# The two lone GRU passes of a four-layer GNN kernel, with their block loops written out

## The reference

```python
gi = a @ W_ih.T + b_ih              # a: the messages summed over each node's edges
gh = h @ W_hh.T + b_hh
i_r, i_z, i_n = split(gi, 3); h_r, h_z, h_n = split(gh, 3)
r = sigmoid(i_r + h_r); z = sigmoid(i_z + h_z)
n = tanh(i_n + r * h_n)
h_new = (1 - z) * n + z * h
```

## Time and profile before

| | us |
|---|---|
| median of 3 runs | 5424.33 (5411.29 to 5428.64) |
| the profiled execution's own time | 5421.28 |
| its span, first to last instruction | 5419.5 |
| the first dense aggregation ends, the first lone GRU begins | 1542.2 |
| its last POOL operation; the next dense stage begins on PE | 1631.8; 1632.7 |
| the last lone GRU begins, with DVE's put(0) | 5326.5 |
| its last DVE operation ends; the output transfer is issued | 5413.4; 5413.7 |

### The profile page before, as it was taken

The page is one execution under the profiler, slowest core; times in us unless marked ns, Lnnn a source line. Parts: engine busy times, 40 slices in busy tenths (PEclk is TensorE's granted clock), DMA queues, the critical chain, the costliest instruction groups (busy, mean ns, idle before and its releaser), DMA issues. The chain is left out here.

```text
span 5419.5 us, 89480 instructions
## 1 busy us (share of the span) xinstructions
PE 3373.2 (62%) x24458; PEld 2518.9 (46%) x24459; DVE 2843.3 (52%) x7137; ACT 944.6 (17%) x2120; POOL 1974.9 (36%) x2334
## 2 busy tenths in 40 slices
PE   4526777776979989989624444444544444445456
PEld 3412333333979988989513332333333333333345
DVE  8976887776553411332324444444554444445565
ACT  3521246664011200001100000000000000000002
POOL 4670000000021111111365655656665555555550
PEclk5558998888999999999655555555555555555557
DMA  3000011112524444544212222222222222222220
GB/s 130 2 3 13 25 47 59 59 59 99 197 70 143 148 153 156 186 158 154 77 41 52 54 53 51 54 52 55 58 57 55 53 53 53 53 52 60 57 59 22
DMA packets 173577, 404.19 MB, mean 75 GB/s; under 512 B 47902, under 2 KB 109481, under 8 KB 172809
## 3 DMA queue, kind: packets, MB, share of 16 engines
q1 hardware_dynamic: 52409, 259.35, 13.4%
q10 hardware_dynamic: 69360, 91.59, 6.2%
q0 software_dynamic: 51680, 51.82, 5.4%
HBM read 359.52 MB, written 43.07 MB: 74 GB/s over the span
## 5 line engine op out<-in xcount | busy, mean ns | idle before, releaser
L704 POOL DMA_INDIRECT scr<-ptable,src_i x1566 | 1520.6, 971 | 1086.0 <-POOLq L702 617.8
L1151 PE MATMUL ps_all<-stat_w,scr 128*128 128x392 fp8e4 x2712 | 615.4, 363 | 255.3 <-PEq L1155 147.2
L964 PE MATMUL ps_all<-arena 128*128 (+1 forms) x1854 | 351.8, 363 | 676.5 <-PEq L962 332.2
L673 POOL COPY late<-late 128x256 f32<-128x256 f32 (+1 forms) x65 | 25.9, 398 | 1980.8 <-POOLq L671 1980.8
L975 PE MATMUL ps_all<-arena 128*128 128x192 bf16 x1854 | 382.3, 360 | 524.1 <-issue 380.7
L967 PE MATMUL ps_all<-sb_w_e,arena 64*128 64x128 f32 x1854 | 530.6, 441 | 233.9 <-issue 233.4
L1042 PE MATMUL ps_all<-scr,arena 128*128 128x192 bf16 x7203 | 611.1, 247 | 66.9 <-PEq L1040 66.9
L1042 PEld LDWEIGHTS ps_all<-scr,arena 128*128 128x128 fp8e4 x7203 | 600.1, 98 | 76.7 <-issue 74.8
L964 PEld LDWEIGHTS ps_all<-arena 128*128 128x128 bf16 x1854 | 227.0, 137 | 809.8 <-issue 798.7
L912 ACT ACTIVATE arena<-arena 128x384 f32<-128x384 f32 x309 | 161.6, 523 | 2499.1 <-ACTq L911 2114.0
L975 PEld LDWEIGHTS ps_all<-arena 128*128 128x128 bf16 x1854 | 230.2, 143 | 695.6 <-issue 687.8
(11 more groups left out here) (305 smaller groups left out, 3620.2 us busy)
## 6 DMA issues: line engine op xcount, KB each, us to landing
arena<-a_dram SPq DMA_DIRECT2D x245, 784.0 KB, 4.4
arena<-low_dram ACTq DMA_DIRECT2D x309, 192.0 KB
a_dram<-arena SPq DMA_DIRECT2D x49, 784.0 KB, 3.3
arena<-in_e32g ACTq DMA_DIRECT2D x309, 96.0 KB
scr<-ptable,src_i POOLq DMA_INDIRECT x1566
arena<-in_e16p SPq DMA_DIRECT2D x1, 13387.5 KB, 35.3
x<-in_x_nm SPq DMA_DIRECT2D x1, 1664.0 KB, 8.3
out_nm<-x SPq DMA_DIRECT2D x1, 1664.0 KB
```

Source lines behind the costliest of these rows:

```text
L704: pool.indirect_dma_start(grow[:, g % RING, j, :], None, ptable, bass.IndirectOffsetOnAxis(ap=src_i[:, g * GC + j:g * GC + j + 1], axis=0) ...
L964: pe.matmul(z[:, j // 2, j % 2 * 3 * H:(j % 2 + 1) * 3 * H], onehotT[:, m, j * P:(j + 1) * P], qsp[:, ds(t, 1), :], start=j % 2 == 0, stop ...
L1151: return pe.matmul(bank_w[i][:, 0:WC], oh_lo[u][:, j, :], oh_hi[u][:, j, :], **{"start": False, "stop": False, **flags})
```

## The change

The loops over pairs of blocks in both lone GRUs are replaced by Python loops that write out all 13 blocks on PE, ACT and DVE. Addresses and semaphore values become constants. The body on each engine changes:

```diff
-WARM = 16
 # ACT
+                turned(0)
+                turned(1)
+                for b in range(NB):
+                    sigmoid((ps_g, ps_g_odd)[b % 2])
+                    if b + 2 < NB:
+                        turned(b + 2)          # copy_uT, copy_hT of block b + 2
+                    tanh()
 # PE
-                    gate_products(k, odd)
-                    for i in range(WARM):
-                        pe.matmul(ps_a[:, 0:P], ident_h[:, :], ident_h[:, :], start=True, stop=True)
-                    turned()
-                    if more:
-                        front(True, True)
+                for b in range(NB):
+                    if b == NB - 1:
+                        pe.wait_ge(s_cdd, 1)
+                        pe.sem_inc(s_cdd, -1)
+                    gate_products(k, b % 2 == 1)
+                    if b + 1 < NB:
+                        turned()
+                    if b + 2 < NB:
+                        front(True, True)
 # DVE
+                def step(ins):
+                    steps[0] += 1
+                    ins.then_inc(s_v, 1)
+                    v.wait_ge(s_v, steps[0])
+                def put(b):
+                    v.tensor_copy(stage[:, :, :], rows(pair, b))
+                    v.tensor_copy(hstage[:, :, 0:H], rows(h, b))
+                    v.tensor_copy(hstage[:, :, H + 2:HX], rows(aux_s, b)).then_inc(s_stg, 1)
+                def block(b):
+                    g = (ps_g, ps_g_odd)[b % 2]
+                    v.wait_ge(s_rz, 1)
+                    v.sem_inc(s_rz, -1)
+                    step(v.tensor_tensor(cand[:, :, :], rz[:, :, 0:H], g[:, :, 3 * H:], ALU.mult))
+                    v.tensor_tensor(cand[:, :, :], cand[:, :, :], g[:, :, 0:H], ALU.add).then_inc(s_cd, 1)
+                    if b + 3 < NB:
+                        stage_free()
+                        put(b + 3)
+                    v.wait_ge(s_th, 1)
+                    v.sem_inc(s_th, -1)
+                    if b == NB - 3:
+                        v.sem_inc(s_cdd, 1)
+                    step(v.tensor_tensor(dif[:, :, :], rows(h, b), cand[:, :, :], ALU.subtract))
+                    step(v.tensor_tensor(dif[:, :, :], dif[:, :, :], rz[:, :, H:], ALU.mult))
+                    v.sem_inc(s_rzf, 1)
+                    if k == 0:
+                        step(v.tensor_tensor(rows(h, b), dif[:, :, :], cand[:, :, :], ALU.add))
+                        v.wait_ge(s_qf, 1)
+                        v.sem_inc(s_qf, -1)
+                        v.tensor_scalar(qblk, rows(h, b), SCALE, None, ALU.mult).then_inc(s_hb, 1)
+                    else:
+                        step(v.tensor_tensor(dif[:, :, :], dif[:, :, :], cand[:, :, :], ALU.add))
+                        step(v.tensor_tensor(rows(x, b), rows(x, b), dif[:, :, :], ALU.add))
+                put(0)
+                for b in (1, 2):
+                    stage_free()
+                    put(b)
+                for b in range(NB):
+                    block(b)
+                v.sem_inc(s_v, -steps[0])
```

More of the change, by code:

```diff
@@ L410, in gnn @@
         s_cd = sem("s_cd")
+        s_cdd = sem("s_cdd")
         s_th = sem("s_th")
@@ L727, in copy_hT, with sigmoid @@
                 act.copy(to[:, :], ps_m[0:HX, :]).then_inc(s_hT, 1)
-            def gates(g):
+            def sigmoid(g):
                 act.wait_ge(s_gt, 1)
@@ L735, in gates, with tanh @@
                 act.activation(rz[:, :, :], g[:, :, H:3 * H], ACT.Sigmoid).then_inc(s_rz, 1)
+            def gates(g):
+                sigmoid(g)
+                tanh()
+            def tanh():
                 act.wait_ge(s_cd, 1)
@@ L741, in gru, with turned @@
                 act.preload_act_table(ACT.Sigmoid)
[L743 to L748, removed]
-                    if more:
[L750 to L759, removed]
+                def turned(b):
+                    copy_uT((uT, uT_odd)[b % 2])
+                    copy_hT((hT, hT_odd)[b % 2])
+                turned(0)
[4 more added lines that the diff above has]
+                        turned(b + 2)
+                    tanh()
             def split(parts, rows, rest, scale=1.0):
@@ L1015, in gru @@
             def gru(k):
-                def block(odd, more=True):
-                    gate_products(k, odd)
-                    for i in range(WARM):
-                        pe.matmul(ps_a[:, 0:P], ident_h[:, :], ident_h[:, :], start=True, stop=True)
-                    turned()
-                    if more:
-                        front(True, True)
                 front(True, True)
@@ L1472, in gru, with rows @@
             def gru(k):
-                def put(b):
-                    link(v.tensor_copy(stage[:, :, :], block_of(pair, b)))
-                    put_rows(b)
+                steps = [0]
+                def rows(buf, b):
+                    return buf[:, b * TB:(b + 1) * TB, :]
+                def step(ins):
+                    steps[0] += 1
+                    ins.then_inc(s_v, 1)
+                    v.wait_ge(s_v, steps[0])
                 def stage_free():
@@ L1480, in stage_free @@
                     v.sem_inc(s_stgf, -1)
-                def block(b, odd, more=True):
-                    if more:
-                        stage_free()
-                        put(b + 2)
-                    candidates(ps_g_odd if odd else ps_g)
-                    mixed(b)
+                def put(b):
+                    v.tensor_copy(stage[:, :, :], rows(pair, b))
+                    v.tensor_copy(hstage[:, :, 0:H], rows(h, b))
+                    v.tensor_copy(hstage[:, :, H + 2:HX], rows(aux_s, b)).then_inc(s_stg, 1)
@@ L1488, in block @@
                     if k == 0:
-                        link(v.tensor_tensor(block_of(h, b), dif[:, :, :], cand[:, :, :], ALU.add))
-                        to_split(b)
-                    else:
-                        add_to_x(b)
+                        step(v.tensor_tensor(rows(h, b), dif[:, :, :], cand[:, :, :], ALU.add))
+                        v.wait_ge(s_qf, 1)
+                        v.sem_inc(s_qf, -1)
+                        v.tensor_scalar(qblk, rows(h, b), SCALE, None, ALU.mult).then_inc(s_hb, 1)
+                    else:
+                        step(v.tensor_tensor(dif[:, :, :], dif[:, :, :], cand[:, :, :], ALU.add))
+                        step(v.tensor_tensor(rows(x, b), rows(x, b), dif[:, :, :], ALU.add))
```

## The result

The changed kernel takes 5383.58 us in the median of five runs (5379.28 to 5393.30), the kernel before 5423.33 (5411.29 to 5428.64): a ratio of 0.9926, with a 95% interval of 0.9908 to 0.9945. The profiled execution after is 5383.6 us long (span 5381.8), that of before 5421.3 (5419.5).

The account below looks back on a forecast made before the run. DVE's queue, with its waits and bookkeeping, was taken as the bound; 20.5 us from the last GRU and 12.4 from the first made 32.9 off 5421.3, so 5388.4 (5391.4 from the median; forecast 5390), range 5377 to 5409.

Parts of the forecast that it names:

- the bounds of the parts: Both lone GRUs together: the parts' limits were said to give 27.6 to 36.6 us less, so 5385 to 5397.
- the tail: Last GRU's final steps, behind mult 12: forecast to save 0.2 us.
- What bounds the old kernel: DVE's queue, not an engine's work: Lone GRUs before the change: DVE's queue, with its waits and bookkeeping, sets 5.8 us a block.
- The step of 0.50: DVE's linked step in the last GRU: 0.57 us with the decrement, taken as 0.50 with the counted wait.
- Last GRU, balance of PE and DVE at 4.05 a block: Last lone GRU: DVE and PE both near 4.0 us, mult 0 to mult 12 48.4 against 69.8.
- 0.5 off for fetching code: Last GRU: 0.5 us struck from the gain of 21 because written-out blocks are more instruction blocks to fetch.
- Prologues unchanged: Stretch before the first mult of each lone GRU: no change, PE at the low clock there.
- First GRU: POOL becomes the bound at 4.85: First lone GRU: POOL paces blocks at 4.85 us, before 5.87, for a gain of 12.4.
- Exclusion of DVE and POOL: Rival, first GRU: SBUF operations hold each other off, 5.45 us a block, total gain 25.7, 5397; 15%.
- The fall of the clock: Rival, PE in both GRUs: without fillers the clock falls, 24 us more in each GRU, 5469; 4%.
- The late-front rival: Rival: put waits for ACT's copy behind a late front, periods near 5.5, 8 us less in all, 5415; 5%.
- Its own signs of being wrong: Last GRU's blocks over 4.6 us, first not paced by POOL, or anything outside both stretches moving over 3 us.

Follow-up runs that it names:

- E2: Kernel before with its three loops over pairs of blocks written out, nothing else: first lone GRU 63.05 us, last 62.76, in all 5423.43.
- E3: Changed kernel with counted steps turned back into wait for 1 and decrement: first GRU 58.97 us, last 50.20.
- E8: Changed kernel with PE transposing three tiles of four in the last GRU from block 3 on: last 44.59 us, first 58.01, in all 5390.91.
- E12: Kernel before with the fillers (unread PE products) dropped, nothing else: mult 0 to mult 12 of last GRU 70.98 us, of first 74.85, in all 4760.27.
- E10: Kernel before with loops written out and fillers dropped: last GRU 62.71 us, first 64.47.
- E1: Changed kernel with the 16 filler products put back behind each block's gate products: first GRU 58.12 us, last 56.92, in all 5403.23.
- E6: Changed kernel with POOL's split in five operations instead of six, its first copy of qblk gone: first GRU 51.44 us, in all 5379.68.
- E7: E6 with POOL's loop of the first GRU also written out: first 49.08 us, last 46.70, in all 5368.35, ratio to the kernel before 0.9891.
- E5: Changed kernel with the put two blocks ahead, before the candidates: first GRU 67.71 us, last 66.26, in all 5407.99.
- E9: Changed kernel with the put two blocks ahead, before the candidates, and ACT's old order: first GRU 60.36 us, last 56.35, in all 4734.05.
- E4: Changed kernel with ACT's old order (sigmoid, tanh, then copies): first GRU 57.86 us, last 47.79, in all 5407.25.
- E11: E7 with unread products where PE would wait ahead of the lone GRUs: 4699.94 us, ratio to the kernel before 0.9887.

## Why the prediction was right, point by point

The profiled execution was forecast at 5388.4 and took 5383.6; 32.9 us were to go, 37.8 went. That is more than the bounds of the parts allowed (36.6; their lower sum is 28.1, not 27.6), and the surplus lies in the last GRU: 24.7 went, 20.5 were forecast, 22 were its limit. The 4.2 us are a longer fall of mult 0 to mult 12 (1.7), the prologue (1.2), a slip in the sum (21.4 and 0.2 are 21.6, not 21: 0.6), the 0.5 for fetching code and the tail (0.2). So the place of the gain and its mechanism were right, and the total came within the stated 5377 to 5409 by the allowance for the spread of the runs. By its own steps:

- *What bounds the old kernel: DVE's queue, not an engine's work.* Right. E2 took 7 us out with no operation changed, by turning a loop into constants, and DVE's rows there close on themselves at 5.33 with the tanh as their only wait.
- *The step of 0.50.* Between 0.47 and 0.57 I took 0.50; 0.46 was measured, and E3 gives 0.10 a step. DVE's block with the tanh needs 3.66 and not 3.84.
- *Last GRU, balance of PE and DVE at 4.05 a block.* This is the term that was mis-sized: 3.91, set by PE (E8). I had PE at 3.97 and the tanh making DVE 0.17 late. From the add to the subtract 1.20 is measured (5353.28 to 5354.48) against 1.11 without the copies, so it is 0.09 late, and with DVE quicker this disappears in the 0.25 between 3.66 and 3.91. Mult 0 to mult 12 fell by 23.1, not 21.4.
- *0.5 off for fetching code.* No run shows this term: the view of waits above has no wait for issue, and PE has no gap. The halt of rows 11, an idle of 0.53 ahead of the third copy of put(1), stands in the kernel before and in E12 (4669.21). In E2 and E10, which have the same straight code there and no loop behind it, that copy starts 0.44 behind the one ahead (5341.49, 4661.13), against 0.83 in the kernel before, and has no idle; the cause was not shown.
- *Prologues unchanged.* Half wrong. PE does run at the low clock there (granted 0.58 from 1537.60 to 1549.90, 0.60 from 5313.00 to 5325.40), but in the last GRU front(0) starts 0.88 behind put(0) and front(1) 4.39; before, 1.36 and 5.31 (E2 has 1.36 and 4.93). So 0.54 of the 1.20 us are the links that I had taken out of every block and not of the puts ahead of the loop, and 0.38 is the halt of rows 11. The other 0.28 is luck: from front(1) to mult 0 the changed kernel takes 7.57 and the one before 7.85, but E1 to E8 spread from 7.0 to 8.2, by how far PE has come when its clock rises: in E2 (7.0) the products of the second tile are the first to take less than 1.06 (0.96), in the changed kernel those of the third (0.80), in E3 (8.2) those of the fourth (0.69). In the first GRU 0.44 of the 0.57 lie between mult 0 and POOL's first copy (4.20 before, 3.76 after), four counted steps. The tail gave 0.43, not 0.2.
- *First GRU: POOL becomes the bound at 4.85.* Right: 4.82, with 0.54 of idle ahead of its copy (E6 and E7 show the bound). 13.1 went, 12.4 were forecast.
- *The rivals.* Exclusion of DVE and POOL (the lock, in the chances) asks for 5.45 a block; 4.82 was measured, and 4.09 in E7, where POOL's 2.5 and DVE's 2.5 of work would sum to 5.0. What the rows below show is a delay: the 512-column copy of 1558.82 ends at 1559.24, 0.28 behind the end of POOL's copy, and that of 1584.60 at 1585.29, 0.28 behind the end of POOL's subtraction. It takes 0.42 in the one case, where POOL's operation has 0.14 left when it starts, and 0.69 in the other, where 0.41 is left; in the last GRU, without POOL, it takes 0.42. What fails is the rival's sum, which let the engines exclude each other for all of an operation's time. From the 0.40 for 256 columns and 0.24 for 64 I estimate that 0.19 of POOL's 0.40 doesn't depend on the columns; whether it is this part that excludes nothing was not shown. The stretch of about 0.9 a block lies in the 0.5 to 1 that I allowed. The fall of the clock did not come: 0.99. But E12 shows that my price of it had a cause: in the old order the fillers were needed (0.80 in its first GRU without them). The late-front rival did not come either, but E5 shows how near it was: with the put two ahead and ACT's new order it is 5.77 a block.
- *Its own signs of being wrong.* The blocks of the last GRU stayed under 4.6, and POOL paced the first. But two stretches outside the GRUs moved by 4.6 and 4.7 us, where I had said that over 3 would count against me. Runs of the unchanged stretch between the GRUs spread by some 30 us, so 3 was too narrow a mark to tell anything.

POOL's rows that go with DVE's copies of 1558.82 and 1584.60 in the changed kernel:

```profile
1558.56 0.40 POOL L673 COPY late<-late 128x256 f32<-128x256 f32 x1 [0.59 <-POOLq L671]
...
1584.34 0.67 POOL L676 TENSOR_TENSOR late<-late,arena 128x256 f32<-128x256 f32 x1 [0.18 <-POOLq L666]
```

The gain of the last GRU, as a ladder of runs: 69.8 before; 62.8 written out (62.7 without fillers too, E10); 56.4 with counted steps and a put without waits (E9, two decisions in one step); 47.8 with the put three ahead, behind the candidates (E4); 46.7 with ACT's new order. In this ladder the fillers are free at 5.33 a block and cost 10.2 at 3.91 (E1). E7, with POOL relieved, beats both kernels.

## What to carry to other kernels

Where no engine is full, time the queue: here a decrement cost 0.10 us (E3), and loop turns with computed addresses 0.6 a block (E2), and taking them out pays until the next engine is dense, so work out that engine's period first. How far ahead a stage is filled and the order in which another engine serves it were one decision here: ACT's new order gave 1.1 us of the last GRU with the put three ahead (E4) and took 9.9 with it two ahead (E5 against E9). Whether unread products pay has to be asked again after each change of density: the same 16 were worth 5 us in the old loop of the first GRU, 1 in that of the last and 1 in the first GRU written out, nothing in the last GRU written out, and minus 10 in the new order.

## What the runs showed of the hardware

The same program takes 5426 us on one chip and 4754 on another. The GRU stretches are alike (46.70 us from mult 0 to mult 12 in the changed kernel, in E7 and in E11). Most of the difference lies in the gather stage between them, from POOL's first indirect transfer to its last: 2602 us in the kernel before on the slower chip, 2001 in E12 on the faster one, 601 of the 661 us by which the two spans differ. POOL waits there ahead of its indirect transfers. POOL's waits there, in the changed kernel on the slower chip and in E12 on the faster one (total us, times, longest):

```profile
POOL scr L704 <- POOLq L702: 618.0, 75, 14.5
```
```profile
POOL scr L704 <- POOLq L702: 83.4, 259, 4.8
```

Few long waits on the one, many short ones on the other; what differs in the chips stays open. The other surprise was the clock: in E12 it fell to 0.51 (4695.60 to 4698.00) within a loop in which PE worked for 4.1 us of each block of 5.85 or 6.33, behind fronts with 2.25 and 1.75 us of idle ahead of them.
